# A fused cross-attention and mixture layer on one core: the norm vectors' load moved from ScalarE's queue into SyncE's, and the last product on zeros halved

## The reference, cut to what matters

```python
def rmsnorm(x, w):
    var = jnp.mean(xf * xf, axis=-1, keepdims=True)
    return (xf * jax.lax.rsqrt(var + EPS)).astype(x.dtype) * w

features_n = rmsnorm(features, fn_w)                 # features: 256 context rows of 1024
Q = rmsnorm(einsum('btd,fd->btf', text, Wq_w) + Wq_b, qn_w)
K = rmsnorm(einsum('bsd,fd->bsf', features_n, Wk_w) + Wk_b, kn_w)
attended = softmax(Q @ K.T * scale) @ features_n
x = x + tanh(g_xattn) * attended                     # text is layernorm(x), x: 4 x 512 x 1024
x = x + tanh(g_ffn) * ffn(layernorm(x))              # ffn: x @ W_base.T + b_base, plus 8 gated rank-16 experts
```

## Time and profile before

| | |
|---|---|
| median of 3 runs | 475.64 us |
| lowest, highest | 475.55, 479.05 us |
| the profiled execution | 475.13 us |
| its span, first to last instruction | 473.3 us |
| TensorE busy | 468.2 us (99%), 2497 records |
| VectorE busy | 357.9 us (76%) |
| ScalarE busy | 173.8 us (37%) |
| bytes read from and written to HBM | 61.93 MB, 22.02 MB |

### The profile page before, as it was taken

The page is one execution under the profiler, slowest core; times in us unless marked ns, Lnnn a source line. Parts: engine busy times, 40 slices in busy tenths (PEclk is TensorE's granted clock), DMA queues, the critical chain, the costliest instruction groups (busy, mean ns, idle before and its releaser), DMA issues.

```text
span 473.3 us, 6973 instructions
## 1 busy us (share of the span) xinstructions
PE 468.2 (99%) x2497; PEld 401.2 (85%) x2497; DVE 357.9 (76%) x746; ACT 173.8 (37%) x349; POOL 119.7 (25%) x107
## 2 busy tenths in 40 slices
PE   8999999999999999999999999999999999999996
PEld 7898999998888888888888888888888888888885
DVE  1687996598979958779977979867786777877632
ACT  5847532341224214126335525243241522315200
POOL 0020501003353443346143306040320403204000
PEclk9999999999999999999999999999999999999999
DMA  8993139958676476487479550311305031040202
GB/s 321 410 409 120 75 92 391 403 182 301 198 260 219 162 259 247 150 295 271 175 267 424 245 177 1 125 54 55 125 0 179 0 134 44 17 162 1 89 1 89
DMA packets 22114, 84.40 MB, mean 178 GB/s; under 512 B 2624, under 2 KB 3904, under 8 KB 19264
## 3 DMA queue, kind: packets, MB, share of 16 engines
q1 hardware_dynamic: 21792, 83.81, 48.2%
q10 hardware_dynamic: 288, 0.15, 0.1%
HBM read 61.93 MB, written 22.02 MB: 177 GB/s over the span
## 4 chain that ended last, share of the span: by engine, by line
PE 99%; DVE 0%; DVEq 0%; issue 0%
PE bank L772 11%; PE bank L776 11%; PE bank L774 11%; PE bank L649 11%; PE bank L685 7%; PE bank L687 7%; PE bank L686 7%; PE bank L745 5%; PE bank L530 4%; PE bank L747 2%; PE bank L671 2%; PE bank L670 2%; PE bank L672 2%; PE bank L724 2%; PE bank L725 2%; PE bank L599 2%
## 5 line engine op out<-in xcount | busy, mean ns | idle before, releaser
L1555 POOL TENSOR_TENSOR small<-small,tiny 128x1 f32<-128x1 f32 (+2 forms) x25 | 21.6, 865 | 165.3 <-DVE small L1186 138.6
L1535 DVE SCALAR_TENSOR_TENSOR xs<-bank,tiny,xs 128x512 f32<-128x512 f32 (+1 forms) x61 | 43.3, 738 | 21.4 <-PE bank L776 15.8
L685 PE MATMUL bank<-xth,gram 128*128 128x512 f32 x144 | 57.3, 398 | 0.0
L687 PE MATMUL bank<-xtl,gram 128*128 128x512 f32 x144 | 56.3, 391 | 0.0
L686 PE MATMUL bank<-xth,gram 128*128 128x512 f32 x144 | 56.1, 390 | 0.0
L772 PE MATMUL bank<-wh_B,zh 128*128 128x512 f32 x116 | 47.0, 405 | 0.0
L772 PE MATMUL bank<-wh_T,zh 128*128 128x512 f32 (+1 forms) x116 | 46.6, 402 | 0.0
L1583 POOL TENSOR_TENSOR sq_sum<-sq_sum,sq 128x512 f32<-128x512 f32 x24 | 32.0, 1335 | 56.6 <-DVE sq L1365 56.6
L776 PE MATMUL bank<-wh_B,zl 128*128 128x512 f32 x116 | 45.6, 393 | 0.0
L774 PE MATMUL bank<-wl_B,zh 128*128 128x512 f32 x116 | 45.4, 391 | 0.0
L776 PE MATMUL bank<-wh_T,zl 128*128 128x512 f32 (+1 forms) x116 | 44.7, 386 | 0.0
(11 more groups left out here) (199 smaller groups left out, 1129.3 us busy)
## 6 DMA issues: line engine op xcount, KB each, us to landing
xst<-x_dram SPq DMA_DIRECT2D x16, 512.0 KB, 4.2
xz<-xt_dram SPq DMA_DIRECT2D x16, 512.0 KB, 7.7
out_dram<-xs SPq DMA_DIRECT2D x14, 512.0 KB, 2.7
xa<-x_dram SPq DMA_DIRECT2D x12, 512.0 KB, 3.8
x<-xa SPq DMA_DIRECT2D x12, 512.0 KB, 2.9
xs<-x SPq DMA_DIRECT2D x12, 512.0 KB, 3.9
wq_raw<-wq_dram SPq DMA_DIRECT2D x8, 512.0 KB, 14.1
t_raw_T<-wb_dram SPq DMA_DIRECT2D x4, 1024.0 KB, 16.6
```

The costliest lines, as they stand in the source:

```text
L685: pe.matmul(acc[:, :], gram[:, g, 0, :], xth[b % 2][:, r, :], start=r == ROWS[j][0], stop=False)
L687: done = pe.matmul(acc[:, :], gram[:, g, 0, :], xtl[b % 2][:, r, :], start=False, stop=r == ROWS[j][-1])
L1535: dve.scalar_tensor_tensor(out=xs[slot][:, cols], in0=bank[n_bank][:, 0:hi - lo], scalar=tg[:, 1:2], in1=xs[slot][:, cols], op0=ALU.mult, ...
```

## The change

The load of `vecs` leaves ScalarE's queue, and is issued by SyncE after the first transfer of `ct_wk01` and before the second. `IDLE` becomes a list of widths: four products of 256 columns and one of 128, in place of five of 256. Nothing else is edited, and no wait is.

```diff
-        IDLE = 5
+        IDLE = [2 * P] * 4 + [P]
...
-            for n in range(IDLE):
-                pe.matmul(bank[T_BANKS[0]][:, 0:2 * P], idle[:, 0:P], idle[:, 0:2 * P], start=True, stop=True)
+            for n in IDLE:
+                pe.matmul(bank[T_BANKS[0]][:, 0:n], idle[:, 0:P], idle[:, 0:n], start=True, stop=True)
...
             for c in range(4):
                 sp.dma_start(ct_wk01[:, :, c, :], front[:, c, :, :]).then_inc(ld_ct[c], 16)
+                if c == 0:
+                    sp.dma_start(vecs[:, :, :], vec).then_inc(ld_vec, 16)
...
-            act.dma_start(vecs[:, :, :], vec).then_inc(ld_vec, 16)
             act.wait_ge(v_idle, 1)
```

## The result

The changed kernel takes 477.05 us (median of 22 runs, 475.95 to 481.81), the kernel before 475.58 us (22 runs, 474.59 to 479.05). The medians are 1.5 us apart; the ratio over all runs is 1.0036, 95% interval 1.0022 to 1.0050, which is 1.7 us: a small loss but one clear of the measurement, where 0.2 us of gain were forecast and 476.7 us was the end of the range. Seven of the 22 runs of the changed kernel took 478.3 us or more, against one of the kernel before. The profiled one took 476.46 us, so its trace shows 1.4 us of loss and nothing of those seven.

What follows compares the result with a forecast made beforehand. TensorE, busy 468.2 of 473.3 us, was taken as the bound; the shorter zeros give 0.21 us, the moved load nothing. From the median, 475.64 - 0.21 = 475.4 us; range 474.6 to 476.7 us.

Steps and rivals of the forecast that it cites:

- the one on the later issue: SyncE's start: second transfer's issue slides from 1.2 to 1.65 us, covered by queued transfers with DMA engines full at 400 GB/s.
- The rival on late vectors: Kernel start: vecs lands between 4.5 and 5.8 us, TensorE gaps behind its zeros; up to 476.1 us; chance 8%.
- give or take 0.1: The two first scalings, waiting for the first transfer and vecs, still start at 4.45 us, within 0.1 us.
- 0.21 us need little room: After the start: later transfers never make TensorE wait, so all of the 0.21 us gain reaches the end.
- The half product: Fifth product on zeros: costs 0.44 us in place of 0.85, k01 about 0.4 us earlier, 0.21 us left at the end.
- the rival that weight loads set its price: Fifth product on zeros: narrow product costs its weight load; 0.18 us saved, 0.09 at the end, 475.5 us; chance 12%.
- the clock's rise: TensorE's start: half speed until about 6.5 us, taken as unchanged, so 0.21 us come out and not 0.42.
- The clock rival: TensorE's start: a gap between 5.2 and 6.5 us keeps the clock low, up to 478.7 us; chance 4%.
- The end: ScalarE's last store: no change expected, bounds -0.8 and +0.6 us; 8% for 474.6 us, 8% for 476.0 us.
- the trace agrees, since no byte disappears by the move: Load of vecs: queues share the 16 engines, so two issuers only save issue time, about 0.43 to 0.46 us.

Runs made afterwards that it cites:

- e1: The changed kernel run again, nothing edited, for a second trace; 477.15 us, ratio 1.0031 to the kernel before.
- e2: Kernel before with only the vecs load moved to SyncE behind the first transfer, five full products on zeros kept; 476.46 us, ratio 1.0021.
- e7: Kernel before with a SyncE wait for GpSimd's constants behind the first transfer, second issued at 1.6 us, no transfer added; 475.41 us, ratio 1.0004.
- e18: Kernel before with SyncE's wait for GpSimd's constants behind the first transfer, no transfer added, run once more; 475.97 us, ratio 1.0001.
- e3: Kernel before with only the fifth product on zeros halved, vecs still loaded early by ScalarE; 475.63 us, ratio 1.0004.
- e14: The kernel before run again, nothing edited, for a second trace of its start; 476.01 us, ratio 1.0004.
- e9: Kernel before with vecs still on ScalarE's queue but issued only after ScalarE's first operation is done, at 2.27 us; 484.15 us, ratio 1.0163.
- e10: Kernel before with vecs issued late by ScalarE (about 2.3 us) and SyncE's pause behind the first transfer, no transfer added; 481.36 us, ratio 1.0105.
- e11: Kernel before with vecs issued late by ScalarE, plus an unneeded SyncE transfer of 160 bytes a partition behind the first; 479.52 us, ratio 1.0082.
- e12: Kernel before with vecs issued late by ScalarE, plus an unneeded SyncE transfer of 512 bytes a partition behind the first; 481.97 us, ratio 1.0128.
- e16: Kernel before with late ScalarE vecs load and SyncE's pause behind the first transfer, no transfer added, run once more; 479.78 us, ratio 1.0091.
- e4: Kernel before with the vecs load placed behind ScalarE's first operation without waiting for it, issued at 1.18 us; 475.11 us, ratio 0.9996.
- e17: Kernel before plus an unneeded second copy of vec into a spare tile, issued by SyncE behind the first transfer; 476.10 us, ratio 0.9992.
- e6: Kernel before plus an unneeded transfer of 512 bytes a partition, issued by SyncE behind the first transfer; 476.23 us, ratio 1.0024.
- e5: Kernel before plus an unneeded transfer of 160 bytes a partition, issued by SyncE behind the first transfer; 475.83 us, ratio 1.0010.
- e15: Kernel before plus an unneeded SyncE transfer of 160 bytes a partition behind the first, run once more; 476.79 us, ratio 1.0022.

## Why the prediction was wrong

*The step that failed* is the one on the later issue: "This is covered by the transfers already queued", and "the second's descriptors are needed then [about 4 us] and no earlier". I took a transfer to be ready for the engines soon after its issue, and the engines to be kept at 400 GB/s by whatever lay queued. In place of that the rate fell to 191 GB/s from 3.6 to 5.6 us (215 in e1, 247 in e2), with three more large transfers issued, and the second one landed 1.9 to 2.4 us late in three traces of the move. TensorE waited 1.0 to 1.2 us for it. A pause of 0.4 us in SyncE's list with nothing added (e7, e18) already sufficed for 0.7 to 1.35 us of lateness, though not for a measurable loss. Why the move makes it later than its own half us stays open. The rows held a hint that I read as harmless: only 16 packets of the first transfer had moved by 2.5 us, 1.8 us after its issue.

*The rival on late vectors* had the right kind of event at the wrong transfer. `vecs` landed where the first transfer had been, 4.51 us against 4.45, well within the forecast of "give or take 0.1" in the first trace; in e1 it was 4.85, outside it. What came late was the transfer behind it. Its upper bound of 476.1 us rested on one late landing that shifts nobody else; here all later transfers moved too.

*"0.21 us need little room"*, and so the transfers after the start were not priced for a delay. Transfers were 1.8 us late and TensorE 0.5, so their room had to be 1.3 us; it was about half a us at 40 us, where the split of the query weights came late, and 0.8 us were lost. From key block 2 to the last product, e1 took 0.9 us longer than the kernel before and e2 0.7.

*The half product* behaved as reckoned: the ten records of L545 run from 1.19 to 5.40 us, 0.42 less than before, the two narrow ones 0.42 us long each, and `k01` starts at 5.20 us. They start 0.21 us apart. That a 128-column product costs half of a 256-column one at half speed holds, and the rival that weight loads set its price falls. But its 0.2 us do not show as time: e3 is at 1.0004 (0.9994 to 1.0014), too wide to rule them out. In the changed kernel they could not show, since TensorE waited for the second transfer whatever the zeros did. The reckoning took the clock's rise to be at 6.5 us in every execution. It lay between about 4.0 us (e3) and 7.4 us (e14). In e3 and e7 the zeros ended before the data, and there a shorter filler gains nothing, so the mean gain is less than 0.21 us by this reckoning; no run measured it.

*The clock rival* (a gap keeps it low) did not occur in the changed kernel: when TensorE resumes at 8.21 us its 24 records take 5.45 us, 0.22 apart, full speed. It did occur where `vecs` came late. In e9 TensorE waited 4.1 us, and behind the wait its records were 0.43 us apart until about 14 us, so the 32 records took 9.7 us in place of 7.5:

```profile
9.12 9.70 PE L600 MATMUL bank<-ct_wk 128*128 128x256 f32 x32 [4.12 <-ACT ct_wk L973]
```

Behind waits of 2.8 to 4.8 us in e10, e11, e12 and e16 they took 8.9 to 10.0 us. The times of these five runs hold that cost besides the wait. *The end* did not move.

*By the Trainium skill* (DMA: Bandwidth & Descriptors, Issuing engines are not separate DMA queues) a second issuer only saves issue time, which is usually small beside the transfer. For `vecs` itself the traces agree: issued by ScalarE at 1.18 us it landed after 3.5 us (e4), and by SyncE at 1.24 us after 3.2 to 3.5 (changed kernel, e1, e2). That the issue time is small did not make it harmless here: about 0.4 to 0.5 us of it put the second transfer about half a us late or more. The prediction's "the trace agrees, since no byte disappears by the move" proved only that the bytes are the same, not when they come.

Summed up: forecast 473.3 - 0.21; the trace has 474.7. The first record of `k01` came 0.42 us earlier, the eight records took 0.34 less by an earlier rise of the clock, the gap before the ninth cost 1.16 between starts, and 0.11 went in the records behind it: together +0.51 at key block 2. Then +0.80 at 40 us, and +0.09 at the end.

## What to carry to other kernels

A queue that looks full does not cover a later issue. In this kernel, whose start hangs on the second landing, every trace with an instruction put between the first two issues had that landing late, by about half a us or more. Judge such an edit by the landings of the transfers behind it, not by that of the transfer moved, and price the whole chain of later loads for the delay. A filler that ends within half a us of the data can't be tuned from one trace, since the clock's rise moved by more than that: from 6.5 to 7.4 us in two traces of the kernel before alone.

## What the runs showed of the hardware

A small load on ScalarE's queue takes no short way past SyncE's: issued at 2.27 us, behind at least three transfers of 512 KB, it landed 5.5 to 7.7 us later in five traces (e9, e10, e11, e12, e16), about when the second to fourth of SyncE's did. From 0.74 us it took 2.4 to 3.5 us. In e16 ScalarE stood idle for 7.8 us before it:

```profile
10.02 0.91 ACT L975 ACTIVATE ct_wk<-ct_wk,vecs 128x256 f32<-128x256 f32 x2 [7.79 <-DMA vecs<-vec_dram]
```

TensorE's clock can fall again in mid-kernel. In the trace of e17 TensorE waited 2.2 us for VectorE at 148 us (behind `xz`, which had waited 2.6 us for its transfer), and the products behind it were 0.43 us apart, half speed, until about 153.3 us. They were 0.22 apart before the wait:

```profile
150.24 1.09 PE L532 MATMUL bank<-ident,px 128*128 128x128 f32 x4 [2.17 <-DVE px L1400]
...
151.98 0.63 PE L689 MATMUL bank<-xtl,gram 128*128 128x512 f32 x1
152.40 0.63 PE L687 MATMUL bank<-xth,gram 128*128 128x512 f32 x1
```

That execution took 478.86 us, the longest of e17's eleven. In e6 the same wait was 1.9 us long, and the products behind it were 0.23 us apart from 151.0 us on, full speed. It also stood in e5, e15, e11 (0.8 us each), e12 (0.7), e7, e18 (0.3) and e9 (1.6), and not in the traces of the kernel before, the changed kernel, e1 and e2. It is a second place where a late transfer reaches TensorE, and may be a source of the runs near 479 us; no run here was made to show that.
